# Attention values copied out unturned, scaled by their inverted sums on loading, and an SP list in a new order

## The chip, the core and the metric

One core of a Trainium2 chip runs the whole program. The metric is the device time of one execution in microseconds; the median of several runs is compared. A profile of one further execution gives the trace.

## What is computed

The input `x` has 8 batches of 1024 tokens with 256 features. `xn` is its layer norm. The result is `x + attention(xn) + linear(xn)`, where the linear part quantises each token of `xn` to 8 bits, multiplies by an int8 matrix and scales back, and the attention is:

```python
q = (x @ Wq.T).reshape(n, s, 16, 16)           # 16 heads of 16
k = (x @ Wk.T).reshape(n, s, 8, 16)            # 8 key heads, each shared by 2 heads
v = (x @ Wv.T).reshape(n, s, 8, 16)
energy = einsum('nqhd,nkhd->nhqk', q, k) + alibi(s, s)   # -|i - j| times a slope for each head
attn = softmax(energy / 4, axis=-1)
out = einsum('nhqk,nkhd->nqhd', attn, v).reshape(n, s, 256) @ Wo.T + bo
```

## The kernel before

**Units.** The work of attention is cut into 64 units: unit `u` is key head `u % 8` of batch `u // 8`, with the two query heads that share it (`e` = 0, 1) and all 1024 tokens. The 64 token tiles of 128 (layer norm, q, k, v, the linear part) are made ahead of the units that need them: eleven at the start, two in each odd unit up to unit 53. Odd units from 9 on also project two tiles of finished attention (`outputs`), whose operands `load_att_t` brings from DRAM. So the code alternates between short even units and longer odd ones; the last odd units make no tiles.

**A unit on TensorE.** A unit has eight steps `c`, one for each block of 128 keys. In a step PE computes four `col_half` results (keys by queries) into a ring of three PSUM banks; ScalarE takes the exp of each out of its bank into `probs`; GpSimd multiplies the diagonal block by ALiBi's share (`weigh_near`); and two steps later `pv_block` multiplies `probs` by the values into `ps_pv`, with a column of ones so that row 16 of each group holds the sum of the exps. Between these PE computes two blocks of row scores (queries by keys, `half_row_block`) into two banks `ps_row`, ahead of their use: in unit `u` the blocks 0 to 7 belong to head 1 of unit `u + 1`, the blocks 8 to 15 to head 0 of unit `u + 2`. VectorE reduces each to the rows' maxima (`reduce_block`), and PE may fill a bank again only when it has been reduced. The maxima go, through GpSimd and a turn on VectorE (`turn_max`), back into the query operand by small DMAs (`place_max`), which PE waits for at the start of the next unit.

**Operands.** q and k are split into three bf16 parts in DRAM (`store_parts`); `load_set` brings the rows of a unit into one of four slots with thirteen DMAs. `load_again` copies 64 of these rows to partitions 64 to 127 (`k_again`, `q_again`), so that `half_row_block` can use both halves of PE at once. The first set of each batch after the first is a *late set* (units 8, 16, ... 56): its last tile is made only three units before. Its loads stand at the end of SP's list of that unit (an odd one) and its `load_again` at the end of the next unit's list (an even one). Its head-0 blocks use `row_block`, which needs no copy.

**Values out.** When a unit's last `pv_block` is done, VectorE turns `ps_pv` into `pv_turned` (`turn_pv`), inverts the sums (`find_rsum`), multiplies (`norm`, on GpSimd in even units) and turns back (`turn_back`); `store_att` puts the result into `att_dram`. `ps_pv` is free for the next unit's first `pv_block` after `turn_pv`. The last batch's tiles are projected by `project_last` in the last two units and at the end, straight into the then unused `ps_row` banks.

**Order.** Nothing is scheduled automatically. Each engine runs its list in the order in which it is written, and waits at semaphores. All DMAs are issued by SP from one list; the order of the calls in its `unit` is the order of issue, and a DMA whose wait is not met holds up everything behind it.

Of the kernel before, what the change touches and what calls it, by code (L numbers as in the profile page):

```python
# [35 lines left out]
P = 128  # L36
# [27 lines left out]
V_COLS = 32  # L64
LN_EPS = 1e-5
# [6 lines left out]
PAIR = 2  # L72
# [20 lines left out]
FIRST_ROWS = K_LOADS + Q_LOADS + ALIBI_LOADS  # L93
# [45 lines left out]
def ring_places():  # L139
# [3 lines left out]
    for u in range(UNITS):  # L143
        f = flags_of(u)
        for c in range(BLOCKS):
            items = [(u, c, e, h) for e in range(GROUP) for h in range(2)]
            if c == 1:
                items += [(u, "outputs", t % PAIR) for t in f["proj"] or f["made"]]
                items += [(u, "qkv", t % PAIR) for t in f["made"]]
            for item in items:  # L150
                places[item] = len(places)
# [38 lines left out]
def build(nc, x, x_t, wqk_t, wv_t, wo_t, wo_last_t, w8_t, w_scale, bias_attn, bias_lin, q_alibi, k_alibi, diag,  # L190
          eye, parts_dram, token_dram, att_dram, out):
    ctx = ExitStack()
    with ctx:
# [58 lines left out]
        rsum = sb("rsum", [P, HALF // TURN])  # L252
        att_normed = sb("att_normed", [P, HALF // 2])
        att_unit = sb("att_unit", [P, HALF // 2])
        att_t = sb("att_t", [P, 2, EC, P])
        att_last = sb("att_last", [P, EC, SEQ])
# [12 lines left out]
        parts_more = parts_more.bitcast(BF16).rearrange("p (b m n) -> p b m n", b=2, m=PARTS)  # L269

# [92 lines left out]
        pv_read = sem("pv_read")  # L363
        rsum_ready = sem("rsum_ready")
        norm_done = sem("norm_done")
        att_unit_ready = sem("att_unit_ready")
        att_stored = sem("att_stored")
        att_t_loaded = [sem(f"att_t_loaded{i}") for i in range(2)]
# [62 lines left out]
        def _(sp):  # L431
# [20 lines left out]
            def load_set(u, slot):  # L452
# [3 lines left out]
                def rows(dst, chunk, row, pick, loaded=set_loaded[slot]):  # L456
                    for at, q_parts, k_parts in PAIRS:
# [16 lines left out]

                pairs = KV_HEADS // (QK_CHUNKS - 1)
                rows(k_set[:, slot, :], QK_CHUNKS - 1, g * HEAD_DIM, "k",
                     first_rows_loaded if u == 0 else set_loaded[slot])
                for e in range(GROUP):
                    rows(q_set[:, slot, e, :], g // pairs, (g % pairs * GROUP + e) * HEAD_DIM, "q",
                         first_rows_loaded if u == 0 and e == 0 else set_loaded[slot])  # L480
# [29 lines left out]
            def store_att(u):  # L510

                wait(sp, att_unit_ready, u + 1)
                for e in range(GROUP):
                    dst = att_dram[bass.ds((u % KV_HEADS * GROUP + e) * HEAD_DIM, HEAD_DIM),
                                   bass.ds(u // KV_HEADS * SEQ, SEQ)]
# [974 lines left out]
```

## Time and profile before

| | |
|---|---|
| median of 3 runs | 1607.19 us (1605.15 to 1607.93) |
| profiled execution | 1606.43 us, of which the span from first to last instruction is 1604.5 us |
| TensorE (PE) busy | 1507.3 us, 94% of the span |
| VectorE (DVE) busy | 1394.1 us, 87% |
| ScalarE (ACT) busy | 1183.8 us, 74% |
| GpSimd (POOL) busy | 1073.4 us, 67% |
| mean granted clock of TensorE | 0.978 of full speed |

Times in the rows are microseconds from the start of the span unless they are marked ns. A line such as L999 is a line of the kernel. Matmuls are pipelined and their ends are modelled, so a busy PE is not PE at its peak. SPq is the queue of SyncE, which issues the DMAs. What stands in brackets is the idle time of the engine before the instruction, and what ended it.

### The profile page before, as it was taken

The page shows a single profiled execution, that of the slowest core. Times are in us where ns is not written, and L with a number is a line of the kernel's source. Part 1 is how long each engine was busy: PE and PEld are TensorE (multiplying, and loading weights), DVE is VectorE, ACT ScalarE, POOL GpSimd, SP SyncE. Part 2 cuts the span into 40 slices and gives each one's busy share as a digit, 9 for nine tenths or more (in the row PEclk, how much of TensorE's full clock was granted, in tenths as well). Part 3 has the DMA queues.
Part 4 walks back from the last instruction along what each step waited for, and adds up shares of the span by engine and source line. Part 5 has one row for each costly group of instructions (what it writes and reads, how often), then busy time and mean ns, then how long its engine had stood idle before and what let it go on. Part 6 is the DMA issues. An engine that isn't in the chain of part 4 may idle for free.

```text
span 1604.5 us, 42517 instructions
## 1 busy us (share of the span) xinstructions
PE 1507.3 (94%) x16284; PEld 584.2 (36%) x16284; DVE 1394.1 (87%) x1698; ACT 1183.8 (74%) x2331; POOL 1073.4 (67%) x1627
## 2 busy tenths in 40 slices
PE   5789989999899998999989999899998999899999
PEld 5323323333333333333333334333333333233333
DVE  6889989999799997999979999799987988899991
ACT  3467777777687775887757887677776777688885
POOL 6457877777688875787757787577785776433332
PEclk9899999999999999999999999999999999999999
DMA  6423233343324333333333333333333332212211
GB/s 169 130 62 84 71 99 79 89 98 84 105 72 106 96 79 98 93 93 101 84 84 95 103 90 90 89 94 97 94 86 85 95 85 69 80 44 70 70 42 61
DMA packets 197291, 140.98 MB, mean 88 GB/s; under 512 B 107040, under 2 KB 165728, under 8 KB 197088
## 3 DMA queue, kind: packets, MB, share of 16 engines
q1 hardware_dynamic: 197088, 138.27, 33.0%
q8 instruction: 129, 2.11, 0.6%
q14 instruction: 74, 0.61, 0.1%
HBM read 81.40 MB, written 35.63 MB: 73 GB/s over the span
## 4 chain that ended last, share of the span: by engine, by line
PE 53%; DVE 31%; issue 8%; SPq 4%; DMA 3%; POOL 0%; ACT 0%; POOLq 0%; ACTq 0%
DVE row_max L999 29%; PE ps_ring L1279 17%; PE ps_pv L1355 15%; PE ps_row L1296 11%; PE ps_ring L1395 4%; PE ps_ring L1415 3%; DMA q_again<-q 2%; PE ps_ring L1398 1%; DVE pv_turned L1039 1%; PE ps_row L1279 1%; PE ps_ring L1409 1%; SPq L497 1%; PE ps_row L1387 1%; SPq L464 0%; DMA base<-x 0%
## 5 line engine op out<-in xcount | busy, mean ns | idle before, releaser
L999 DVE TENSOR_REDUCE row_max<-ps_row 128x1 f32<-128x1024 f32 x1024 | 1199.2, 1213 | 153.8 <-PE ps_row L1298 138.5
L1171 ACT ACTIVATE probs<-ps_ring 128x512 f32<-128x512 f32 x2048 | 1083.7, 601 | 284.8 <-PE ps_ring L1279 282.3
L1279 PE MATMUL ps_ring<-q,k 122*32 122x512 bf16 x8192 | 639.2, 385 | 5.6 <-DMA q<-neg_max_t 4.7
L762 POOL TENSOR_TENSOR probs<-probs,near 128x256 f32<-128x256 f32 x512 | 374.2, 731 | 368.5 <-ACT probs L1171 362.8
L1355 PE MATMUL ps_pv<-probs,v_unit 128*32 128x512 f32 x4096 | 537.9, 601 | 0.0
L1279 PEld LDWEIGHTS ps_ring<-q,k 122*32 122x32 bf16 x8192 | 216.5, 95 | 511.7 <-ACT probs L1171 324.6
L1296 PE MATMUL ps_row<-k,q 64*128 64x512 bf16 x944 | 329.7, 390 | 68.1 <-DMA q_again<-q 43.2
L1298 PE MATMUL ps_row<-k_again,q_again 64*128 64x512 bf16 x944 | 329.6, 390 | 0.0
L1296 PEld LDWEIGHTS ps_row<-k,q 64*128 64x128 bf16 x944 | 83.9, 93 | 362.9 <-issue 197.8
L1355 PEld LDWEIGHTS ps_pv<-probs,v_unit 128*32 128x32 f32 x4096 | 125.2, 110 | 55.1 <-issue 9.1
L1298 PEld LDWEIGHTS ps_row<-k_again,q_again 64*128 64x128 bf16 x944 | 83.8, 93 | 0.0
L817 POOL CAST parts<-qk 128x384 bf16<-128x384 f32 x53 | 26.6, 502 | 83.4 <-ACT qk L1180 83.4
L1395 PE MATMUL ps_ring<-xn_t,wqk 128*128 128x128 f32 x636 | 79.9, 275 | 0.5 <-ACT probs L1171 0.5
L1395 PEld LDWEIGHTS ps_ring<-xn_t,wqk 128*128 128x128 f32 x636 | 77.0, 192 | 2.5 <-ACT probs L1171 1.3
L1039 DVE STREAM_TRANSPOSE pv_turned<-ps_pv 128x512 f32<-128x512 f32 x64 | 45.2, 706 | 28.4 <-PE ps_pv L1355 28.4
L809 POOL TENSOR_SCALAR xq_t<-xround 128x256 bf16<-128x256 f32 x53 | 57.3, 1081 | 4.5
L801 POOL TENSOR_SCALAR xround<-xt_step 128x256 f32<-128x256 f32 x53 | 57.0, 1075 | 4.5
L689 POOL TENSOR_TENSOR parts<-rest,parts 128x384 bf16<-128x384 f32 x59 | 54.1, 917 | 7.2 <-ACT parts L1127 3.0
L1177 ACT ACTIVATE v_all<-ps_ring 128x128 f32<-128x128 f32 x53 | 14.7, 277 | 58.5 <-PE ps_ring L1398 58.5
L1415 PE MATMUL ps_ring<-wo,att_t 128*128 128x256 f32 x224 | 57.4, 382 | 0.0
L1279 PE MATMUL ps_row<-k,q 120*32 120x512 bf16 x640 | 45.3, 390 | 11.7 <-issue 8.9
L819 POOL TENSOR_TENSOR rest<-qk,parts 128x384 f32<-128x384 f32 x53 | 48.5, 916 | 4.3
(84 smaller groups left out, 1009.1 us busy)
## 6 DMA issues: line engine op xcount, KB each, us to landing
parts_dram<-parts SPq DMA_DIRECT2D x59, 288.0 KB, 3.3
q_again<-q SPq DMA_DIRECT2D x63, 256.0 KB, 3.4
token_b<-token_dram SPq DMA_DIRECT2D x53, 256.0 KB, 4.0
q<-parts_dram SPq DMA_DIRECT2D x128, 96.0 KB
k<-parts_dram SPq DMA_DIRECT2D x256, 32.0 KB
q<-parts_dram SPq DMA_DIRECT2D x128, 64.0 KB
att_dram<-att_unit SPq DMA_DIRECT2D x126, 64.0 KB
att_t<-att_dram SPq DMA_DIRECT2D x56, 128.0 KB, 2.9
```

Of the source, the lines that this page charges most:

```text
L762: pool.tensor_tensor(here, here, near[:, u % KV_HEADS, :].rearrange("p (e n) -> p e n", e=GROUP), ALU.mult).then_inc(weighted, 1)
L801: pool.tensor_scalar(xround[:, :], xt_step[:, 1, :, :].rearrange("p c n -> p (c n)"), Q_MAX, ROUND, ALU.min, ALU.add).then_inc(xt_rounded, 1)
L809: pool.tensor_scalar(xq_t[:, t % TURNED, :, :].rearrange("p c n -> p (c n)"), xround[:, :], -ROUND, -Q_MAX - 1, ALU.add, ALU.max).then_inc ...
L999: dve.tensor_reduce(row_max[:, par, e, qb:qb + 1], ps_row[qb % 2][:, :], AX_X, ALU.max, negate=True).then_inc(row_max_found, 1)
L1039: dve.transpose(pv_turned[:, :], ps_pv[:, :]).then_inc(pv_read, 1)
L1171: act.activation(probs[:, c % PBUFS, e, h * HALF:(h + 1) * HALF], ring_bank(u, c, e, h), ACT.Exp, scale=SCALE).then_inc(ring_freed, 1)
L1279: mm = pe.matmul(to[at, :], weights[:, at], moving, start=start, stop=stop)
L1296: pe.matmul(ps_row[qb % 2][:, 0:HALF], q_set[0:ROW_K, slot, e, at], k_set[0:ROW_K, slot, 0:HALF], start=True, stop=True)
L1298: pe.matmul(ps_row[qb % 2][:, HALF:SEQ], q_again[ROW_K:2 * ROW_K, u % AGAIN, e, at], k_again[ROW_K:2 * ROW_K, u % AGAIN, :], start=True, s ...
L1355: mm = pe.matmul(ps_pv[32 * j:32 * j + 32, :], v_unit[:, par, c, :], probs[:, c % PBUFS, j // 2, (j % 2) * HALF:(j % 2 + 1) * HALF], start ...
L1395: pe.matmul(bank[:, m * P:(m + 1) * P], wqk[:, c, m * P:(m + 1) * P], xn_t[:, t % TURNED, c, :], start=(c == 0), stop=(c == EC - 1))
L1415: mm = pe.matmul(bank[:, EMBED:2 * EMBED], att_t[:, t % 2, c, :], wo[:, c, :], start=(c == 0), stop=(c == EC - 1))
```

## The change

- ScalarE copies `ps_pv` to `att_raw` as it is (`keep_pv`); `store_att` stores that with its row of sums. `load_sums` brings the sums back spread over 128 partitions, VectorE inverts them (`find_rsum`, before block 13 of the next unit), `store_rsum` stores them. The two tiles to be projected are loaded together (`load_att_t`), with the inverted sums broadcast (`load_att_r`), and GpSimd multiplies (`share`) in step 0 of the projecting unit. The turns and `norm` are left only for the last unit; the last batch's values are multiplied on VectorE (`share_last`).
- On SP, `load_again` of a late set moves near the top of the next unit's list, and late sets use `half_row_block` like the others. `row_block`, now for the first units alone, uses 64 rows in place of 120, and the rows that it needs of set 0 are loaded first. `place_max(0, 0)` and `load_again(1, 1)` move up in the list at the start.
- In step 1 of odd units `qkv_whole` stands before `outputs`, on PE and ScalarE.

```diff
@@ SP: functions
-                wait(sp, att_unit_ready, u + 1)
-                for e in range(GROUP):
...
+                sp.wait_ge(pv_read, u + 1)
+                sp.dma_start(att_dram[u // KV_HEADS, u % KV_HEADS].rearrange("e h r n -> (e h r) n"),
+                             att_raw[:, u % 2, :]).then_inc(att_stored[u % 2], 16)
+            def load_sums(u):
+                sp.wait_ge(att_stored[u % 2], 16 * (u // 2 + 1))
+                wait(sp, rsum_ready, u - 1)
+                sp.dma_start(sums[:, u % 2, :],
+                             att_dram[u // KV_HEADS, u % KV_HEADS, :, :, HEAD_DIM, :].rearrange(
+                                 "e h (k n) -> (e h) k n", n=SUMS)).then_inc(sums_loaded[u % 2], 16)
+            def store_rsum(u):
+                sp.wait_ge(rsum_ready, u + 1)
+                sp.dma_start(rsum_dram[u // KV_HEADS, u % KV_HEADS].rearrange(
+                    "e (k n) -> (e k) n", n=SUMS), rsum[:, u % 2, :]).then_inc(rsum_stored[u % 2], 16)
+            def load_att_r(t):
+                b, at = t // BLOCKS, t % BLOCKS * P
+                wait_units(rsum_stored, (b + 1) * KV_HEADS)
+                for c in range(EC):
+                    sp.dma_start(att_r[:, c, :],
...
@@ SP: at the start
             load_set(2, 2)
+            load_again(1, 1)
             sp.dma_start(wo[:, :, :], wo_t.rearrange("(c p) n -> p c n", p=P)).then_inc(
...
             load_token(PREP_AHEAD)
-            load_again(1, 1)
+            place_max(0, 0)
             load_again(2, 2)
-            place_max(0, 0)
@@ SP: unit
                     load_xt(u + 2 + PREP_AHEAD)
+                if u + 2 < UNITS and late_set(u + 2):
+                    load_again(u + 2, (u + 2) % SETS)
+                if f["prev"]:
+                    store_att(u - 1)
                 if f["row_set"] and not late_set(u + 3):
                     next_set(u + 3)
-                if u % PAIR == 1:
-                    store_att(u - 1)
                 for t in f["normed"]:
                     store_token(t)
...
+                if f["prev"]:
+                    load_sums(u - 1)
...
                 if not f["last"]:
                     place_max(u + 1, (u + 1) % SETS)
-                if f["prev"] and u % PAIR == 0:
-                    store_att(u - 1)
-                for t in f["next_att"]:
-                    load_att_t(t, t % 2)
+                for t in f["next_att"][:1]:
+                    load_att_t(t)
+                if f["prev"] and not f["last"]:
+                    store_rsum(u - 1)
                 if f["row_set"]:
                     if late_set(u + 3):
                         next_set(u + 3)
                     else:
                         load_again(u + 3, (u + 3) % SETS)
-                if u + 2 < UNITS and late_set(u + 2):
-                    load_again(u + 2, (u + 2) % SETS)
+                for t in f["next_att"][:1]:
+                    load_att_r(t)
@@ GpSimd
+            def share(t):
+                pool.wait_ge(att_t_loaded, 16 * 2 * EC * (t // PAIR + 1))
+                pool.tensor_tensor(att_t[:, :, :], att_t[:, :, :], att_r[:, :, :],
+                                   ALU.mult).then_inc(att_t_ready, 1)
...
-                    if c == 3 and f["prev"] and u % PAIR == 0:
-                        norm(u - 1)
+                    if c == 0:
+                        for t in f["proj"][:1]:
+                            share(t)
@@ VectorE
+                dve.wait_ge(sums_loaded[u % 2], 16 * (u // 2 + 1))
+                wait(dve, rsum_stored[u % 2], 16 * (u // 2))
+                dve.reciprocal(rsum[:, u % 2, :], sums[:, u % 2, :]).then_inc(rsum_ready, 1)
...
                     for i in (2 * c, 2 * c + 1):
+                        if i == 13 and f["prev"]:
+                            find_rsum(u - 1)
                         if i < BLOCKS and f["row_heads"] >= 1:
                             reduce_block(u + 1, (u + 1) % 2, 1, i)
                         if i >= BLOCKS and f["row_heads"] >= 2:
                             reduce_block(u + 2, u % 2, 0, i - BLOCKS)
-                        if i == 3 and f["prev"]:
-                            turn_pv(u - 1)
...
+                    if c == 3 and u == UNITS - 2:
+                        share_last(0, P)
@@ ScalarE
+            def keep_pv(u):
+                act.wait_ge(pv_done, BLOCKS * (u + 1))
+                wait(act, att_stored[u % 2], 16 * (u // 2))
+                act.activation(att_raw[:, u % 2, :], ps_pv[:, :], ACT.Copy).then_inc(pv_read, 1)
...
+                    if c == 1 and f["prev"]:
+                        keep_pv(u - 1)
@@ TensorE
-                        if not late_set(u + 2):
-                            wait_again(u + 2)
-                    if late_set(u + 2):
-                        row_block(u + 2, (u + 2) % SETS, 0, i - BLOCKS)
-                    else:
-                        half_row_block(u + 2, (u + 2) % SETS, 0, i - BLOCKS)
+                        wait_again(u + 2)
+                    half_row_block(u + 2, (u + 2) % SETS, 0, i - BLOCKS)
...
-            project_last(1, P - GROUP * HEAD_DIM, 2)
             pv_block(UNITS - 1, (UNITS - 1) % 2, BLOCKS - 1)
-            for i in range(3, BLOCKS):
+            for i in range(BLOCKS):
                 project_last(1, P - GROUP * HEAD_DIM, i)
```

## Rows read from the trace of the kernel before

**Rows 1.** The chain of work that ended last, shares by engine.
```profile
PE 53%; DVE 31%; issue 8%; SPq 4%; DMA 3%; POOL 0%; ACT 0%; POOLq 0%; ACTq 0%
```
**Rows 2.** Timeline of VectorE in an even unit: start, duration, instruction.
```profile
552.32 4.73 DVE L999 TENSOR_REDUCE row_max<-ps_row 128x1 f32<-128x1024 f32 x4 [0.28 <-PE ps_row L1298]
...
559.83 0.23 DVE L1046 RECIPROCAL rsum<-pv_turned 128x16 f32<-128x16 f32 x1
...
562.56 2.36 DVE L999 TENSOR_REDUCE row_max<-ps_row 128x1 f32<-128x1024 f32 x2 [0.29 <-PE ps_row L1298]
...
567.57 2.35 DVE L999 TENSOR_REDUCE row_max<-ps_row 128x1 f32<-128x1024 f32 x2 [0.28 <-PE ps_row L1298]
569.84 0.43 DVE L1065 STREAM_TRANSPOSE att_unit<-att_normed 128x256 f32<-128x256 f32 x1
```
**Rows 3.** List of waits: total, times, longest.
```profile
PE ps_row L1296 <- DMA q_again<-q: 43.2, 7, 7.2
```
**Rows 4.** Windows: length, busy engines, clock, DMA; sum of the seven late pairs.
```profile
537.29:583.54 46.25, 45.58 (x494) 17.70 (x492) 43.27 (x53) 36.52 (x73) 35.41 (x54) 1.00 0.34 91
1452.45:1494.77 42.32, 41.66 (x458) 13.70 (x456) 40.23 (x41) 34.60 (x67) 14.82 (x25) 1.00 0.25 69
...
sum 377.79, PE 330.84 PEld 126.25 DVE 300.44 ACT 254.79 POOL 238.30; mean PE 47.26 PEld 18.04 DVE 42.92 ACT 36.40 POOL 34.04
```
**Rows 5.** Timeline of SP's queue around a late set.
```profile
595.50 0.62 SPq L468 DMA_DIRECT2D k<-parts_dram  x1
...
601.74 0.83 SPq L488 DMA_DIRECT2D k<-k_alibi  x2
...
603.50 0.45 SPq L555 DMA_DIRECT2D xt<-x_t  x1
...
622.09 0.59 SPq L499 DMA_DIRECT2D q_again<-q  x1
```
**Rows 6.** Timeline of TensorE in the same stretch.
```profile
608.27 1.04 PE L1279 MATMUL ps_row<-k,q 120*32 120x512 bf16 x16
...
625.91 0.60 PE L1296 MATMUL ps_row<-k,q 64*128 64x512 bf16 x1 [6.99 <-DMA q_again<-q]
```
**Rows 7.** Timeline of SP's queue: a set's first DMA in a quiet stretch.
```profile
1469.48 0.69 SPq L468 DMA_DIRECT2D k<-parts_dram  x1
```
**Rows 8.** Windows at the end of that set; DMA share is the last but one.
```profile
1478.50:1479.50 1.00, 1.00 (x20) 0.29 (x12) 1.00 (x2) 0.69 (x3) 0.81 (x3) 1.00 0.15 57
1479.50:1480.00 0.50, 0.50 (x9) 0.10 (x2) 0.50 (x2) 0.50 (x2) 0.00 (x0) 1.00 0.05 16
```
**Rows 9.** DMA issues: count, size, median us from issue to landing.
```profile
q_again<-q SPq DMA_DIRECT2D x63, 256.0 KB, 3.4
...
token_dram<-token SPq DMA_DIRECT2D x53, 2.0 KB, 3.9
```
**Rows 10.** Timelines of ScalarE and SP in the even unit of rows 2.
```profile
556.57 2.06 ACT L1171 ACTIVATE probs<-ps_ring 128x512 f32<-128x512 f32 x4 [0.48 <-PE ps_ring L1279]
...
556.90 0.69 SPq L468 DMA_DIRECT2D k<-parts_dram  x1
...
564.95 0.35 SPq L568 DMA_DIRECT2D token_b<-token_dram  x1
```
**Rows 11.** Timeline of GpSimd and TensorE in an odd unit that makes no tiles.
```profile
1490.25 0.73 POOL L762 TENSOR_TENSOR probs<-probs,near 128x256 f32<-128x256 f32 x1 [1.17 <-ACT probs L1171]
...
1491.87 1.99 PE L1415 MATMUL ps_ring<-wo,att_t 128*128 128x256 f32 x8
```
**Rows 12.** Timelines of SP and TensorE at the start of unit 0.
```profile
64.70 0.34 SPq L568 DMA_DIRECT2D token_b<-token_dram  x1
...
67.72 3.17 SPq L506 DMA_DIRECT2D q<-neg_max_t  x4
...
72.12 1.04 PE L1279 MATMUL ps_ring<-q,k 122*32 122x512 bf16 x8 [4.74 <-DMA q<-neg_max_t]
```
**Rows 13.** Timeline of TensorE at the end.
```profile
1595.14 2.43 PE L1387 MATMUL ps_row<-wo,att_last 96*128 96x256 f32 x10
```

More of the change, by code:

```diff
@@ L92 @@
 ALIBI_LOADS = 2
-FIRST_ROWS = K_LOADS + Q_LOADS + ALIBI_LOADS
+NEAR_PAIRS = tuple(pair for pair in PAIRS if pair[0] < ROW_K)
+FAR_PAIRS = tuple(pair for pair in PAIRS if pair[0] >= ROW_K)
+FIRST_ROWS = 2 * len(NEAR_PAIRS) + ALIBI_LOADS
 def made_unit(t):
@@ L454, in load_set, with rows @@
                 g, tok = u % KV_HEADS, (u // KV_HEADS) * SEQ
-                def rows(dst, chunk, row, pick, loaded=set_loaded[slot]):
-                    for at, q_parts, k_parts in PAIRS:
+                def rows(dst, chunk, row, pick, pairs=PAIRS, loaded=set_loaded[slot]):
+                    for at, q_parts, k_parts in pairs:
                         use = q_parts if pick == "q" else k_parts
@@ new lines, in wait_units, with heads_of, load_att_t @@
+            def wait_units(stored, units):
+                for i in range(2):
+                    sp.wait_ge(stored[i], 16 * len(range(i, units, 2)))
+            def heads_of(c):
+                return slice(c * (KV_HEADS // EC), (c + 1) * (KV_HEADS // EC))
+            def load_att_t(t):
+                b, half, at = t // BLOCKS, t % BLOCKS // (BLOCKS // 2), t % (BLOCKS // 2) * P
+                wait_units(att_stored, (b + 1) * KV_HEADS)
+                if t >= PAIR:
+                    wait_filled(sp, projected_unit(t - PAIR), "outputs", 1)
+                for c in range(EC):
+                    sp.dma_start(att_t[:, c, :],
+                                 att_dram[b, heads_of(c), :, half, 0:HEAD_DIM, at:at + PAIR * P].rearrange(
+                                     "g e d n -> (g e) d n")).then_inc(att_t_loaded, 16)
@@ L850, in unit @@
             def unit(u, f):
-                t = u + PREP_AHEAD
+                turned = u + PREP_AHEAD
                 for c in range(BLOCKS):
@@ L1077, in unit @@
                             reduce_block(u + 2, u % 2, 0, i - BLOCKS)
-                        if i == 3 and f["prev"]:
-                            turn_pv(u - 1)
-                        if i == at_sums and f["prev"]:
-                            find_rsum(u - 1)
-                        if i == at_norm and f["prev"] and not apart:
-                            norm(u - 1)
-                        if i == SLOTS - 3 and apart:
-                            turn_back(u - 1)
                     if c == 1:
```

182 lines of the change are left out of this document (90 added, 92 removed).

## The prediction

> **What bounds the kernel now.** I read the chain of work that ended last first: 53% of it is TensorE, 31% VectorE [rows 1]. In steady work TensorE and VectorE alternate: PE fills two `ps_row` banks, VectorE reduces them, and a bank must be read before it is filled again. Eight blocks undisturbed would take 10.02 us, twice the 5.01 us for four between 562.56 and 567.57 [rows 2]; with `turn_pv` and `find_rsum` among them, from 552.32 to 562.56, they take 10.24. So VectorE's extra work costs only 0.22 us there, since part of it falls into idle time that the handshake leaves anyway.
>
> Then the list of waits: PE waited 43.2 us for `q_again`, seven times, up to 7.2 [rows 3]. Windows of two units say where: an ordinary pair takes 46.25 us, a pair late in the kernel that makes no tile 42.32, and the seven pairs in which a batch's first set arrives late 377.79 together [rows 4]. Six ordinary pairs and one short one are 319.82, so the seven lose 58.0 us, 8.3 each. SP's list and PE's tell how [rows 5, 6]: the late set's loads are issued from 595.50 to 602.6, but its second copy follows only at 622.09, behind another set, `place_max`, `store_att`, `load_att_t` and the next set's copy; PE, which reached the blocks at about 618.9, starts them at 625.91, and its matmuls then run 0.60 us instead of 0.39 for a while.
>
> Last, the landing of a set. Its thirteen DMAs begin at 1469.48 and traffic ends at about 1479.7 [rows 7, 8]; in the tail only 0.15 of 16 engines are busy, 2.4 engines. So a set lands 10.2 us after its first issue, and a few engines set that.
>
> **The change, part by part.** *Late copies.* `load_again` of the late set now stands near the top of SP's list of the even unit, but it waits for the set. The set's loads come behind `store_rsum` in the unit before, which adds one small issue of 0.45 us: first issue 595.95 [rows 5], landed 10.2 later, 606.15. SP is there by 604.4 and waits, as everything behind it does. The k copy's issue takes 0.59 like the q copy's, so the q copy starts at 606.8 and lands 3.4 later (median, [rows 9]): 610.2. Now the even unit's head-0 blocks need that copy too, at about 608.1 (the old block, which read the set directly, ran at 608.27 [rows 6], less 0.2 for VectorE's relief). PE waits 2.1 us; bounds 0.7 (set landed when SP gets there) and 3.1 (the copy takes 3.8, as at 622.09 to 625.9, and its set 0.6 more). I add 0.6 for slow matmuls after the stall (0 to 1.7).
>
> *Values out.* `turn_pv`, `norm` and `turn_back` leave VectorE. In an odd unit they hide behind the tile work of PE, so they give nothing. In an even one they give 0.22 [rows 2] and about 0.2 for `turn_back`, whose 0.43 us at 569.84 stands ahead of a reduction that PE waits for: together -0.42 a pair. ScalarE gets a copy of 128x512; like an exp of that size it takes 0.6, placed after the exps of c = 1, where ScalarE has idle time: four exps take 2.06 us [rows 10] of the 2.5 that a step of c lasts. A ring bank comes free up to 0.25 late: 0.1 taken (0 to 0.25). GpSimd loses a product in even units and gains, in odd ones, `share` on 128x512; it waits for others in most steps, so only PE's wait for `share` counts (below).
>
> *Sums back.* This is the new wait. `find_rsum` moves to just before block 13 and waits for `load_sums`. Everything queued behind it on VectorE waits too, first the reduction of block 13, and PE's block 15 waits for that; so what it lasts is PE's. The reciprocal itself (0.23) costs about 0.2 in each unit, 0.4 a pair. Now its data. In an even unit the copy of the values starts when the exp begun at 556.57 is done, 557.1, ends at 557.7; `store_att` takes 0.4 of SP's time, so `next_set` starts at 558.3, 1.4 later than before [rows 10]. `load_sums` comes behind its thirteen DMAs, 8.05 later, 566.35 (as the token load at 564.95 stood to 556.90). If it goes through the engines of the tail, it lands with the set, 558.3 + 10.2, plus 0.4 for its own small packets: 568.9. VectorE arrives at 567.57 + 1.18 - 0.2 = 568.55 [rows 2]. Stall 0.4. Bounds: 0, if it does not queue behind the tail; 1.7, if it takes 3.9 us from its issue as the token store does, the row nearest to it in packet size [rows 9]. I take 0.4, nearest to the set's own landing, which rows show most directly. An ordinary pair so costs -0.42 + 0.4 + 0.1 + 0.4 = +0.5 (-0.1 to +2.0); 24 of them, +12.
>
> The Trainium skill (DMA: Bandwidth & Descriptors, "Why a DMA increments its semaphore by 16 and not by 1") says that an SP transfer is split over as many engines, up to 16, as divide the outermost dimensions of both sides, and takes the lowest-numbered. Loads with two or three parts outermost would then sit on engines 0 to 2, which the 0.15 share bears out, and the sums, four rows outermost, on 0 to 3, behind them. By that rule the stall is the 0.4 taken; without it the sums could land at once, and the sum would be 10 us lower.
>
> In a late pair the set behind the copies starts at about 608.0 and its sums land at 608.0 + 10.2 + 0.4, and 0.6 for the copies' data ahead of it: 619.2. VectorE arrives a pair later than above, 568.55 + 46.25, plus the stalls of 2.1 and 0.6: 617.5. It waits 1.7. New loss of a late pair: 2.1 + 0.6 + 1.7 and the common +0.1 = 4.5 for 8.3 before; seven give -26.6.
>
> `place_max` of an even unit now comes behind `store_att` and `load_sums` too, at about 567.1. From its first issue to PE's start it took 4.4 us where PE stood waiting, 67.72 to 72.12 [rows 12], so 571.5. PE's next unit starts two steps of c after that of block 12, about 571.5 and the stall of 0.4. I take 0 (0 to 0.5). `store_rsum` and `load_att_r` stand at the list's end; once a batch `load_att_r` must see the last sums stored (about 3.9 [rows 9]), and behind it wait `store_out` and the next unit's x loads. SP then stood before `store_att`, which waits for the copy 6.4 us into the unit anyhow: 0.
>
> *Projection.* PE makes qkv first, so `share` is covered by it in units that make tiles. Five odd units at the end make none: GpSimd's product of c = 0 ends at 1490.98 there, `share` takes twice its 0.73, to 1492.4, and PE wanted the operands at 1491.87 [rows 11]. 0.6 each, and about 1 more where the batch's last sums are only just stored: +4.
>
> *Start.* Fewer first rows let PE begin 2 to 3 us earlier, but SP's list governs unit 0. `place_max` (67.72) came 3.0 after the token load (64.70), behind two pairs of copies [rows 12]. The first blocks' 64 rows instead of 120 change nothing by themselves: the columns are the same. One pair moves ahead of the token's store and delays it by 1.2, the other behind: -1.5 (-3 to 0).
>
> *End.* Eight of the last products instead of five stand behind the last values, at 0.24 an instruction with two each [rows 13], less what no longer stands between earlier matmuls; and `share_last(0)`, 128x1024 on VectorE, delays the first projection by about its 1.2 us (a reduction of that size takes 1.18). Together +2 (0 to 4).
>
> **Sum.** -26.6 + 12 - 1.5 + 4 + 2 = -10.1. The profiled execution took 1606.43 us (span 1604.5); its sum is 1596.3. The median of the runs is 0.8 above it, so I forecast 1597 for a median.
>
> **Rivals.** *The sums come late (slower).* At 3.9 us from issue the even units' stall is 1.7, 1.3 more than taken; over 31 pairs that is +40, 1637. It decides from a stall of 0.7 on, where the ten microseconds are spent. For it: the small packets, and a load of values stored in the same unit. Against it: the set in front lands at 568.5, and nothing else is queued there.
>
> *The rows' cover holds (much faster).* Copies land when PE needs them and sums pass the tail: late pairs keep 0.5, 7 x 7.8 = 55 gained, ordinary ones cost +0.1, +2; with start, projection and end 1607.2 - 55 + 2 + 4.5 = 1559. For it: the copies leave some 15 us earlier than the 622.09 of before [rows 5]. Against it: they cannot leave before 606.15.
>
> *It cancels (no change).* One late wait becomes three smaller ones, stalls of 2.7 and 2.6 in the late unit leave 5.9 of 8.3: -17 + 12 + 4.5, 1607. For it: VectorE and PE stand in lockstep, so neither stall hides the other.
>
> **Chances.** Forecast 0.38 (1588 to 1603), sums late 0.34, cover 0.15, cancels 0.13. What a measurement can tell from no change is about 0.2%, 3.2 us: faster 0.38 + 0.15 = 0.53, same 0.13, slower 0.34. The range reaches to 1565, which leaves out half of the third case, and to 1630, leaving out about a third of the second.
>
> **What the profile after would show.** PE's waits for `q_again`: seven of about 2 us, where 43.2 stood. VectorE waiting for `sums` before `find_rsum`: 0.4 in even units, nothing in odd ones. Pairs of 46.7 in place of 46.25. ScalarE about 38 us busier, VectorE less busy by what it turned (0.43 a unit for `turn_back` alone [rows 2]), with hardly any gain from that. Were VectorE's wait over 0.7, or PE's for the copies over 4, I would be wrong by sign; were PE to wait for `set_loaded` at the start of odd units, I would have placed `place_max` wrongly.

## The result, and the profile of the changed kernel

The changed kernel takes 1646.3 us (median of four runs, 1638.6 to 1653.0) where the kernel before took 1607.6 in the same comparison: a ratio of 1.024, 95% interval 1.019 to 1.029. It is 2.4% slower; the forecast was 1597, range 1565 to 1630. The profiled execution of the changed kernel took 1638.56 us, with a span of 1636.8 where that of before was 1604.5. It was the quickest of the four: the two traces differ by 32.3 us, the medians by 38.7.

The page of the changed kernel, busy time by engine and the chain that ended last, stands against [rows 1]:

```profile
PE 1512.9 (92%) x15948; PEld 578.4 (35%) x15948; DVE 1328.3 (81%) x1542; ACT 1214.6 (74%) x2394; POOL 1095.7 (67%) x1624
...
PE 31%; DVE 17%; SPq 17%; POOL 13%; issue 11%; DMA 9%; ACT 2%; POOLq 0%; ACTq 0%; DVEq 0%
```

VectorE is 65.8 us less busy, as the change says, and the kernel is slower all the same. SP's queue, 4% of the chain before, is now 17%, and DMA went from 3% to 9%: the chain runs through transfers. The list of waits (total, times, longest) says which; the last line is from the kernel before:

```profile
DVE rsum L1099 <- DMA sums<-att_dram: 66.8, 31, 18.4
PE ps_row L1348 <- DVE row_max L1060: 59.4, 65, 3.7
...
PE ps_row L1348 <- issue: 21.3, 7, 3.5
...
PE ps_ring L1461 <- POOL att_t L815: 5.1, 5, 2.5
```
```profile
PE ps_row L1296 <- DVE row_max L999: 11.0, 39, 1.9
```

VectorE waited 31 times for the sums: in thirty even units 48.4 us together, from 0.71 to 3.40, and 18.4 in the last unit, where nobody waits for it. The second line is what PE paid for it: 59.4 us of waits for a reduction, of which the kernel before had 11.0 as well, and the other 48.4 are what VectorE waited in the even units. The third, named "issue" here, stands where late sets are first used: seven waits for late copies, 3.0 each where [rows 3] had 6.2. The fourth is PE's wait for `share`. One even unit in detail, on SP, VectorE and PE:

```profile
714.95 0.69 SPq L481 DMA_DIRECT2D k<-parts_dram  x1
...
722.23 0.59 SPq L539 DMA_DIRECT2D sums<-att_dram  x1
```
```profile
721.64 3.61 DVE L1060 TENSOR_REDUCE row_max<-ps_row 128x1 f32<-128x1024 f32 x3
726.38 0.25 DVE L1099 RECIPROCAL rsum<-sums 128x16 f32<-128x16 f32 x1 [1.13 <-DMA sums<-att_dram]
```
```profile
727.76 0.39 PE L1348 MATMUL ps_row<-k,q 64*128 64x512 bf16 x1 [1.16 <-DVE row_max L1060]
```

The set's first load goes out at 714.95, the sums at 722.23, VectorE asks for them at 725.25 (726.38 less 1.13), 10.30 us after the set's first issue, and gets them 11.43 after it. The 1.13 us are PE's as well, 1.16, behind the reduction that VectorE could not start. In most other even units VectorE came at the same 10.30, and in all thirty the sums landed 11.0 to 12.8 us after the first issue. At the end of the kernel, with no set ahead, the same load took no more than 2.05 us from issue to use (SP and VectorE):

```profile
1610.76 0.55 SPq L539 DMA_DIRECT2D sums<-att_dram  x1
```
```profile
1612.81 0.25 DVE L1099 RECIPROCAL rsum<-sums 128x16 f32<-128x16 f32 x1 [18.37 <-DMA sums<-att_dram]
```

By pairs (windows; as in [rows 4], an odd unit and the even one behind it, here cut where `ps_pv` is read): an ordinary one, a late one and one without tiles:

```profile
735.11:782.40 47.29, 45.73 (x494) 17.57 (x494) 41.30 (x49) 37.50 (x76) 36.23 (x54) 1.00 0.39 104
782.40:836.68 54.28, 47.16 (x494) 17.64 (x494) 41.33 (x48) 37.60 (x76) 35.92 (x54) 0.97 0.36 95
...
1519.43:1562.90 43.47, 41.43 (x456) 13.33 (x454) 37.96 (x36) 35.60 (x69) 14.62 (x25) 1.00 0.27 78
```

Cut where a unit's `ps_pv` is read (the same place in both traces), the two traces part as follows. Twenty pairs that make tiles and are not late: +31.6 us, 1.6 each. Seven late pairs: -9.4. The last four pairs: +9.9. Start -0.2, end +0.4. Sum +32.3, the difference of the spans. The same kernel profiled once more, in a run of 1644.3 us (e17), parts in +33.4, -11.3, +12.2, +3.4 and +0.4: of the 5.7 us that its span is longer, 3.6 are the start. Late pairs still lose 7.0 us each against ordinary pairs of before (46.25, the first of the seven 45.26), where they lost 8.4. In the pair of the second row, on SP, PE and in two windows,

```profile
801.14 0.62 SPq L481 DMA_DIRECT2D k<-parts_dram  x1
...
812.89 0.59 SPq L518 DMA_DIRECT2D q_again<-q  x1
```
```profile
816.43 0.37 PE L1348 MATMUL ps_row<-k,q 64*128 64x512 bf16 x1 [2.96 <-issue]
...
827.88 0.39 PE L1348 MATMUL ps_row<-k,q 64*128 64x512 bf16 x1 [3.67 <-DVE row_max L1060]
```
```profile
826.00:829.00 3.00, 1.12 (x14) 0.38 (x17) 2.51 (x4) 0.35 (x1) 1.00 (x1) 0.95 0.37 99
829.00:832.00 3.00, 3.00 (x24) 0.63 (x16) 1.15 (x2) 1.72 (x4) 0.80 (x2) 0.50 0.68 188
```

PE waits 2.96 us for the copy, then 3.67 behind VectorE's wait for the sums (the copies had pushed back the next set, and the sums with it), and after that wait the granted clock is 0.50 of full speed (1.2 GHz) for some 3 us.

### The profile page after: what moved, and what is told of

Its sections match the earlier page's. It is cut to its first block, busy times and chain, and to the rows that moved or that the text cites. A ratio compares the mean times of both kernels' runs of the same rounds, so it can differ in the third digit from the quotient of the medians.

```text
span 1636.8 us, 41809 instructions
## 1 busy us (share of the span) xinstructions
PE 1512.9 (92%) x15948; PEld 578.4 (35%) x15948; DVE 1328.3 (81%) x1542; ACT 1214.6 (74%) x2394; POOL 1095.7 (67%) x1624
## 4 chain that ended last, share of the span: by engine, by line
PE 31%; DVE 17%; SPq 17%; POOL 13%; issue 11%; DMA 9%; ACT 2%; POOLq 0%; ACTq 0%; DVEq 0%
DVE row_max L1060 15%; PE ps_ring L1331 9%; PE ps_pv L1407 8%; DMA sums<-att_dram 6%; PE ps_row L1348 5%; SPq L477 5%; SPq L481 4%; POOL probs L822 4%; PE ps_ring L1441 3%; SPq L485 3%; PE ps_ring L1461 2%; DMA k<-k_alibi 2%; SPq L507 1%; SPq L525 1%; POOL parts L754 1%
## 5 line engine op out<-in xcount | busy, mean ns | idle before, releaser
L1348 PE MATMUL ps_row<-k,q 64*128 64x512 bf16 x1000 | 346.4, 389 | 94.2 <-DVE row_max L1060 59.4
L1350 PE MATMUL ps_row<-k_again,q_again 64*128 64x512 bf16 x1000 | 346.6, 389 | 0.0
L1348 PEld LDWEIGHTS ps_row<-k,q 64*128 64x128 bf16 x1000 | 88.9, 93 | 391.4 <-issue 226.8
L1350 PEld LDWEIGHTS ps_row<-k_again,q_again 64*128 64x128 bf16 x1000 | 89.1, 93 | 0.0
L1099 DVE RECIPROCAL rsum<-sums 128x16 f32<-128x16 f32 x63 | 15.6, 247 | 66.8 <-DMA sums<-att_dram 66.8
L849 POOL TENSOR_TENSOR xn_t<-xt_step,token_b 128x256 f32<-128x256 f32 x53 | 45.7, 863 | 4.2
L844 POOL TENSOR_TENSOR xt_step<-xt,token_b 128x256 f32<-128x256 f32 x53 | 47.3, 893 | 0.0
```

What stands on the lines that cost most here:

```text
L1348: pe.matmul(ps_row[qb % 2][:, 0:HALF], q_set[0:ROW_K, slot, e, at], k_set[0:ROW_K, slot, 0:HALF], start=True, stop=True)
L1350: pe.matmul(ps_row[qb % 2][:, HALF:SEQ], q_again[ROW_K:2 * ROW_K, u % AGAIN, e, at], k_again[ROW_K:2 * ROW_K, u % AGAIN, :], start=True, s ...
```

## Experiments

Medians are of the runs of each kernel; the ratio is to the kernel before on the same chip, with its 95% interval.

| run | median us | ratio |
|---|---|---|
| e1 sums inverted before block 15 | 1610.9 | 1.002 (1.001 to 1.003) |
| e2 sums loaded inside the set | 1600.4 | 0.996 (0.994 to 0.998) |
| e3 sums left out | 1596.4 | 0.993 (0.991 to 0.996) |
| e4 before, late copies alone | 1568.9 | 0.976 (0.973 to 0.978) |
| e5 before, copies up, old block | 1573.2 | 0.980 (0.977 to 0.982) |
| e7 e2 with the old block | 1613.9 | 1.003 (1.002 to 1.005) |
| e8 e2 with the maxima inside too | 1595.5 | 0.992 (0.991 to 0.994) |
| e9 e2, inverted before block 9 | 1608.1 | 1.000 (0.998 to 1.001) |
| e10 before, copies behind the maxima | 1549.8 | 0.964 (0.962 to 0.966) |
| e11 before, copies ahead of the maxima | 1557.8 | 0.969 (0.967 to 0.971) |
| e12 e8 with the copies as in e10 | 1593.0 | 0.990 (0.987 to 0.994) |
| e13 before, start alone | 1613.8 | 1.003 (1.002 to 1.004) |
| e14 before, blocks of 64 rows alone | 1612.3 | 1.004 (1.002 to 1.005) |
| e15 e10 with the start's moves | 1551.7 | 0.965 (0.964 to 0.967) |
| e16, e18 changed, blocks of 120 rows | 1639.7, 1641.6 | 1.020 (1.019 to 1.022), 1.022 (1.020 to 1.024) |
| e17 changed, again | 1645.4 | 1.023 (1.021 to 1.026) |

**The stall on the sums.** My theory: it is the loss. Rival: it hides another. Three edits of the changed kernel take it away in different ways.

```diff
@@ e1, VectorE
-                        if i == 13 and f["prev"]:
+                        if i == 15 and f["prev"]:
@@ e2, SP: load_set, called by next_set with the unit whose sums it is to load
                     rows(k_set[:, slot, :], QK_CHUNKS - 1, g * HEAD_DIM, "k")
+                    if between is not None:
+                        load_sums(between)
                     for e in range(GROUP):
@@ e3, SP: unit
-                if f["prev"]:
+                if u in (1, 2):
                     load_sums(u - 1)
@@ e3, VectorE: find_rsum
-                dve.wait_ge(sums_loaded[u % 2], 16 * (u // 2 + 1))
+                dve.wait_ge(sums_loaded[u % 2], 16)
```

e3 scales by old sums; it is there for its time alone.

> Changed kernel, but VectorE inverts the sums before block 15 instead of before block 13. Theory (the sums are late for VectorE): it arrives two reductions, about 2.45 us, later, that is 12.75 us after the set's first issue where it came at 10.30; the sums were there after 11.0 to 12.8. So of the 48.4 us that VectorE waited in thirty even units about 4 stay, and the slow matmuls behind the longer stalls go too: 1590 to 1597 us. Rival (the stall only hides another loss: place_max, the copy on ScalarE or the longer list on SP would be late next): the time stays above 1625 and another wait of about 1 us in each even unit takes the place of this one.

> Changed kernel, but load_sums is issued inside the set, behind its five k loads and ahead of its eight other DMAs, some 5 us earlier than before. Theory: the sums then land well before VectorE comes at 10.30 us after the set's first issue, its wait of 48.4 us falls to under 3 except where no set is issued ahead of them, and the time is 1588 to 1597. Rival (what is late is the round trip through DRAM itself, or the added transfers slow the set): the waits shrink by less than half, or PE waits longer for the sets, and the time stays above 1615.

> Changed kernel with the sums loaded only in units 1 and 2; every later unit inverts what lies there, so the shares are those of old sums. It prices the loads and VectorE's wait for them together. Theory: 48.4 us of waits go, and with them the slow matmuls behind the longer ones, some 8 pairs at 1.5 to 2 us: 1575 to 1590. Rival (the loss lies in ScalarE's copy, in share or in the list): above 1625.

All three kernels lose the stall wholly (in e1 and e2 VectorE waits for the sums only in the last unit, in e3 once, 2.3 us in unit 2, where it still loads them), and are 35 to 50 us faster than the changed one. In e3, without the load and its wait, ordinary pairs take 46.3: what is left of the values' way costs a pair 0.1 us. VectorE's relief does show in even units: from a unit's first column matmul to the next unit's they take 20.13 us for 20.26 before. Odd units, where the turns had been hidden behind tile work and the inversion now stands among the reductions, take 26.18 for 25.98. But each run stays above its theory's range, because something else is late next. In e3 that is the late pairs, which still lose 5.4 us (waits for copies of 3.1 and slow matmuls behind them), and the start (below). In e1 the stores of the inverted sums come some 2 us later, and with them the late set, whose loads stand behind `store_rsum`: PE waits for late copies 38.0 us instead of 21.3, and for `share` 11.3 instead of 5.1. Waits of e1:

```profile
PE ps_row L1348 <- issue: 38.0, 7, 6.8
...
PE ps_ring L1461 <- POOL att_t L815: 11.3, 5, 3.2
```

Waits of e2:

```profile
PEld ps_ring L1334 <- DMA q<-neg_max_t: 23.6, 26, 2.1
...
DVE rsum L1102 <- DMA sums<-att_dram: 18.3, 1, 18.3
...
PE ps_ring L1334 <- DMA q<-neg_max_t: 7.9, 12, 1.4
```

In e2 it is the maxima: PE waits for `place_max` at the start of odd units. In the changed kernel the stall covered that (0.3 us in all). e8 tests it, e9 where the sums' delay comes from.

```diff
@@ e8, on top of e2, SP: load_set, in even units
+                if ahead is not None:
+                    place_max(ahead, ahead % SETS)
                 if u >= SETS - 1:
                     load_alibi(u, slot)
@@ e9, on top of e2, VectorE
-                        if i == 13 and f["prev"]:
+                        if i == 9 and f["prev"]:
```

> Changed kernel with load_sums inside the set, and in even units place_max also inside it, ahead of the two ALiBi loads and the token load. In the run with the sums inside the set VectorE no longer waited for them, but PE's engine and its weight loads waited 7.9 and 23.6 us for the maxima at the start of odd units, and ordinary pairs still varied from 46.3 to 47.5. Theory (the maxima are what is late next): those waits fall under 5 us together, ordinary pairs take 46.3 and the time is 8 to 12 us lower than with the sums alone inside, 1588 to 1593. Rival (the variation is that of the clock or of the transfers themselves): within 3 us of 1600.

> Changed kernel with load_sums inside the set, but VectorE asks for the sums before block 9, some 5.0 us sooner, so that it shows when they land: it comes about 5.2 us after the set's first issue, 2.6 after the issue of the sums. Theory (the sums were late because they lay behind the rest of the set; nearly alone they took 2.05 us at the end of the kernel): they land 2.0 to 2.8 us after their issue, VectorE waits less than 0.3 in most even units, and the time is within 6 us of the run before block 13, 1595 to 1606. Rival (4 us from issue to landing is what such a small load takes anywhere): VectorE waits 1.4 us in each even unit, and the time is 1625 to 1645.

e8: the weight loads' waits for maxima fall from 23.6 us to 7.7, PE's from 7.9 to 2.7, even units in ordinary pairs all take 20.1, and 4.9 us are gained, half of what I expected: twenty ordinary pairs gained 6.4 in the profiled runs, but PE's waits for `share` grew from 5.8 to 8.1 and the last four pairs took 2.5 more. e9: in 18 of the thirty even units the sums were there when VectorE asked, 2.6 us or less after their issue; in 12 it waited, 15.7 us together, and got them 2.05 to 3.07 us after their issue. Behind the whole set it was 2.8 to 4.9, 4.2 in the mean. The theory holds for the landing, though the waits were more than expected and the time lies above its range. The wait of e9, in which 18.5 is the last unit's:

```profile
DVE rsum L1102 <- DMA sums<-att_dram: 34.8, 14, 18.5
```

**The late copies.** In the changed kernel they gave 9.4 us instead of 26.6. Theory: the sums behind them took the rest. So that part alone, in the kernel before:

```diff
@@ e4, SP: unit, near its top; e5 has this edit alone
+                if u + 2 < UNITS and late_set(u + 2):
+                    load_again(u + 2, (u + 2) % SETS)
                 if f["row_set"] and not late_set(u + 3):
                     next_set(u + 3)
...
-                if u + 2 < UNITS and late_set(u + 2):
-                    load_again(u + 2, (u + 2) % SETS)
@@ e4, PE: late sets on half_row_block, as in the change
```

> Kernel before with one part of the change alone: load_again of a late set near the top of the next unit's list, and late sets on half_row_block. Nothing of the sums. Theory (of a late pair's loss in the changed kernel only the 3.0 us wait for the copies belongs to the copies, the rest to the sums behind the next set): late pairs lose 3 to 4 us in place of 8.3, the time is 1570 to 1581. Rival (the copies ahead of the next set cost a late pair some 7 us by themselves, through that set and the unit that waits for it): 1593 to 1603.

> Kernel before with load_again of a late set near the top of the next unit's list and nothing else: its head-0 blocks keep row_block, which reads the set itself. With half_row_block added (the run with the late copies alone) late pairs still lost 3.7 us, of which 2.1 are PE's wait for the copies. Theory (the change of block made that wait; without it the copies are needed only a unit later): late pairs lose about 0.5 us, what four steps of row_block took more (2.61 against 2.50 us each), so some 22 us less than that run: 1544 to 1552. Rival (SP, standing at the top of its list for the set, makes what is behind it late, the maxima above all): 1558 to 1569.

> Changed kernel with load_sums inside the set (as in the run of that name) and row_block kept for the head-0 blocks of late sets. Theory: the late pairs lose PE's wait of 3.1 us for the copies and the slow matmuls behind it, 31 us in all: 1567 to 1574. Rival (in a late unit the set behind the copies, and the maxima behind that set, are late next, and take half of it back): 1580 to 1592.

e4 is 2.4% faster than before, 1 us under its theory's range: late pairs lose 3.0 us, of which 2.1 are the wait for the copies:

```profile
PE ps_row L1296 <- issue: 14.6, 7, 3.0
```

So a part of the change gains 39 us alone, and is buried in a whole that loses 39. But my theory that the copies only had to be taken off PE's path fell in e5 and e7: both lie above even their rivals' ranges, e7 14 us above its partner e2, e5 4 us above e4 (their intervals just overlap). Waits of e5:

```profile
PE ps_ring L1279 <- DMA q<-neg_max_t: 20.9, 8, 5.3
```

One of the eight is the first unit's; the others, 15.6 us together, are new. SP, at the top of its list, stands for the late set, and everything behind comes late, the maxima above all. With `half_row_block` PE waited for the copies meanwhile and saw little of it (2.1 us in e4). In e7 the waits for the maxima are 32.0 us in all.

So the copies belong neither at the top (SP stands) nor at the end (they leave at 622.09, [rows 5]), but in between. The next three move them there:

```diff
@@ e10, kernel before, SP: unit (removed at the list's end)
                 if not f["last"]:
                     place_max(u + 1, (u + 1) % SETS)
+                if u + 2 < UNITS and late_set(u + 2):
+                    load_again(u + 2, (u + 2) % SETS)
@@ e11: the same two lines ahead of place_max
@@ e12: e8, with late sets as in e10 and load_again where place_max stood
```

> Kernel before with one call moved: load_again of a late set stands directly behind place_max of the next unit, ahead of store_att, load_att_t and the other set's copy; its head-0 blocks keep row_block. Theory (at the list's top the copies make SP stand for the set and the maxima come late; at its end they come 7 us late themselves; in between neither does): the copies are issued about 6 us sooner than in the kernel before, 614.9 and 615.5 where they were 621.5 and 622.1, and land at 619 to 619.6, PE comes at 618.9 and waits up to 0.7 us; no wait for the maxima. Late pairs lose 0.5 to 1.5 us instead of 8.3: 1554 to 1563. Rival (wherever they stand, copies and maxima of that unit share a transfer time that comes to some 3 us): 1567 to 1575, like the two runs with the copies at the top.

> As the run with the copies behind the maxima, but directly ahead of place_max. Theory: the copies then land at about 617, before PE wants them at 618.9; the maxima go out 1.2 us later, from 613.4, and are there at about 617.8, when PE wants them at 618.1; late pairs lose about 0.5 us: 1551 to 1560, not over 3 us from the run with the copies behind. Rival (the copies' 384 KB delay the maxima behind them by 2 us or more): PE waits 1 to 3 us for the maxima in late units, 1562 to 1575.

> Changed kernel with the sums inside the set, the maxima inside it in even units, and late sets as in the run of the kernel before with the copies behind the maxima (row_block for head 0, load_again where place_max stood). Theory (with its three waits taken away the values' new way costs almost nothing and gives nothing): ordinary pairs 46.3, late pairs 46.9 to 48, about 5 us for share at the end; 1562 to 1572, some 8 us above the kernel before with the copies so placed. Rival (the values' way has a cost of its own that the waits hid): over 1580.

e10 is 3.6% faster than before, by one call moved, and beats both kernels. A window of a late pair, and what is left of its waits:

```profile
745.78:792.37 46.59, 46.13 (x541) 18.61 (x540) 43.37 (x55) 36.50 (x72) 35.51 (x54) 1.00 0.37 93
```
```profile
PE ps_ring L1279 <- DMA q<-neg_max_t: 5.4, 1, 5.4
...
PEld ps_row L1296 <- DMA q_again<-q: 2.7, 3, 1.2
...
PE ps_row L1296 <- DMA q_again<-q: 1.3, 2, 0.7
```

The wait of 5.4 is the first unit's. Late pairs lose 0.5 us, PE waits for the copies only twice, 1.3 us together, and the granted clock stays at full speed (2.4 GHz) from 76 us to the end of the span. The median lies 4 us below the theory's range. In e11 the maxima wait behind the copies (PE 11.6 us, 4.5 of it in the first unit): its expected time came, but 8 us from e10 where I said at most 3, so the rival's mechanism is there too, at about 1 us a pair. e12 misses: 1593 for 1562 to 1572. The sums and their store stand ahead of the copies, they leave later, and PE waits for them again:

```profile
PE ps_row L1353 <- DMA q_again<-q: 15.8, 6, 3.1
```

Counted from where `ps_pv` is read at the start of the odd unit, its copies leave 1.6 to 3.3 us later than those of e10, and its late pairs lose 4.4 us. So the values' new way has a cost besides the stall after all: what it adds to SP's list delays what is behind. That is the rival's answer, at least in late units. Of the 47.5 us between the profiled runs of e12 and e10 the late pairs are 27.2, the last four pairs, with their waits for `share`, 10.8, the start 5.5 and ordinary pairs 3.6. The new way is not all of the 27.2: late sets use `row_block` with 64 rows here, as in e7, and e14 below prices that at 0.7 a pair.

**The start.** It was forecast at -1.5 and is -0.2 in the profiled run, but 3 to 4 us in most other profiled runs with the same start.

```diff
@@ e14, kernel before, PE: row_block, and k_set alike (e13 has this, the first rows first, and SP's moves)
-                q = q_set[0:SET_K, slot, e, qb * P:(qb + 1) * P]
+                q = q_set[0:ROW_K, slot, e, qb * P:(qb + 1) * P]
...
@@ e15: e10, with load_again(1, 1) and place_max(0, 0) moved up
@@ e16, e18: changed kernel, with SET_K here again and the first loads in the old order
```

> Kernel before with the start of the change alone: near rows of the first set ahead of its far rows, row_block on 64 rows, load_again(1, 1) and place_max(0, 0) further up. The forecast took -1.5 us (-3 to 0). Theory (the first unit waits for its maxima, which go out sooner): PE's wait of 4.7 us for the first maxima falls under 2 and the time is 1604 to 1606.5. Rival (the time until the first set's rows decide, and that differs more from run to run than by this): no difference that three rounds can tell, within 2 us of 1607.4.

> Kernel before with row_block on 64 rows instead of 120 and nothing else (it serves the three first blocks of eight at the start and the head-0 blocks of late sets). In the run with the start alone TensorE's granted clock stayed at 0.50 from 35 to 80 us, and 42.0 us lay between its first row block and its first column block, where the kernel before rose to 1.00 at 43 us and took 34.9, a wait of 4.7 for the maxima among them; and a step of c with row_block in late units took 2.81 us instead of 2.61. Theory (the 64 rows do both): the clock stays low here too, the start takes 39 to 43 us between the same two blocks, late pairs 0.5 to 1 us more, and the time is 1612 to 1619. Rival (the clock hangs on the order of the loads and the earlier start): clock and late steps as in the kernel before, 1605 to 1609.

> The run of the kernel before with the copies behind the maxima (1549.8), and of the start only the two moves in SP's list: load_again(1, 1) and place_max(0, 0) further up, with blocks of 120 rows. Theory: PE's wait of 5.4 us for the first maxima shrinks by what the moves bring place_max forward, 1 to 3 us, and nothing else changes: 1546.5 to 1549. Rival (the copy that now stands ahead of the token's store delays the token load, and with it the maxima behind): 1549.5 to 1552.

Both e13 and e14 are 5 to 6 us slower than before, so the 64 rows alone do it; of e13's two expectations neither came. In the profiled run of e14, the quickest of its six, the start takes 1.2 us more and the late pairs 4.7; in that of e13 3.3 and 5.2. Two ways show. First the clock, in windows of the start of the kernel before and of e14 (the third number from the right):

```profile
50.00:55.00 5.00, 4.67 (x55) 2.32 (x52) 5.00 (x6) 2.15 (x8) 3.49 (x5) 1.00 0.44 133
```
```profile
50.00:55.00 5.00, 5.00 (x38) 2.31 (x31) 3.51 (x4) 1.07 (x3) 2.03 (x4) 0.50 0.43 131
```

It is at 1.2 GHz when the first row block starts, in all traces. With 120 rows it is at full speed by 42 to 45 us in all eight, 4 to 7 us after that start; with 64 by 61 or 62 us in three (the changed kernel, e1, e14) and by 80 or 81 in the other eight. In e14 it takes 37.2 us from the first row block to the first column block, not the 39 to 43 expected, for 34.9 before. Second, in late units, weight loads and matmuls of one step, before and in e14:

```profile
608.06 0.32 PEld L1279 LDWEIGHTS ps_row<-k,q 120*32 120x32 bf16 x8
```
```profile
609.50 0.55 PEld L1279 LDWEIGHTS ps_row<-k,q 64*32 64x32 bf16 x16 [0.42 <-issue]
...
612.31 0.12 PEld L1279 LDWEIGHTS ps_row<-k,q 64*32 64x32 bf16 x8 [0.42 <-issue]
```

The 120-row weights are loaded from 608.06, 0.21 ahead of their matmuls at 608.27 [rows 6]; those of 64 rows begin only with their matmuls, 609.50. A step takes 2.81 us where it took 2.61, and late pairs lose 0.7 more. e15 gives the rival's answer: the moved copy goes out ahead of the token's store, and the first maxima come no earlier (PE waits 6.1 us for them, 5.4 in e10); nothing is gained.

> Changed kernel with row_block on 120 rows and the first set loaded in the old order; all else as changed. Theory (64 rows at the start keep the clock low, for 25 to 45 us, and differently from run to run): from the first row block to the first column block it takes 30 to 33 us instead of 37.5 in the profiled run and 42 in six others, the time is 1636 to 1642. Rival (what the low clock costs is what PE would have waited for maxima anyway): 1644 to 1649, as changed.

> The changed kernel itself, once more, beside the run with blocks of 120 rows. Its four times lay between 1638.6 and 1653.0, those of the kernel with 120 rows between 1637.2 and 1642.0. Theory (64 rows keep the clock low at the start, for 25 us in the profiled run, for 42 in six other kernels with the same start): the median lies 4 to 8 us above that with 120 rows on the same chip, and from first row block to first column block it takes 37 or 42 us. Rival (the spread comes from the stalls on the sums, in both alike): within 3 us of each other.

> The changed kernel with blocks of 120 rows and the old order of the first loads, once more, beside the changed kernel on the same chip. Theory: 4 to 8 us under the changed kernel, its times within 6 us of each other. Rival: within 3 us of it, and as widely spread.

First row block and first column block of e17 and of e18, on PE:

```profile
35.07 1.90 PE L1331 MATMUL ps_row<-k,q 64*32 64x512 bf16 x16 [6.50 <-issue]
...
77.06 1.04 PE L1331 MATMUL ps_ring<-q,k 122*32 122x512 bf16 x8
```
```profile
38.39 1.90 PE L1323 MATMUL ps_row<-k,q 120*32 120x512 bf16 x16 [10.44 <-issue]
...
72.18 1.04 PE L1323 MATMUL ps_ring<-q,k 122*32 122x512 bf16 x8 [3.23 <-DMA q<-neg_max_t]
```

That is 42.0 us against 33.8, less the 3.3 by which the 64 rows let PE begin sooner. In e16 it is 35.3, not the 30 to 33 expected, with 5.7 of it a wait for the maxima, against 37.5 and 0.3 in the first trace of the changed kernel: part of what the slow clock costs is time in which PE would have waited, as e16's rival says. In time it should be some 5 us between e17 and e18; measured are 4, and 7 between the changed kernel and e16, with intervals that overlap. So its size in the changed kernel stays open, and so does the cause of the spread of the changed kernel's runs, which is there with 120 rows too in e18 (1637.7 to 1648.0).

## Why the prediction was wrong, step by step

- **What bounds the kernel**: right. PE and VectorE alternate; the seven late waits were worth 8.4 us each, and e10 gets nearly all of it back.
- **Values out**: right in size. Without the stall the forecast's terms for an ordinary pair make +0.1; e3 measured 46.3 for 46.25, and in its parts too (even units 0.13 shorter, odd ones 0.20 longer) it came as the terms have it.
- **Sums**: the step that failed, by its size. "Stall 0.4" was 1.6 in the mean of thirty units, the smallest 0.71. VectorE's arrival was right: 10.25 us after the set's first issue forecast, 10.30 measured. Wrong was the landing, 10.2 for the set, taken from one late in the kernel with little other traffic [rows 7, 8], and 0.4 for the sums' own packets, 10.6 together; they were there after 11.0 to 12.8, 11.7 in the mean. The 0.4 stands in no row. Even in the last units, which make no tiles, the sums took 11.0 to 11.2, and 11.2 to 12.8 in units with more traffic; that the traffic is the reason is likely, but no run tests it. The order behind it was right: e2 and e9 show that what stands ahead of the sums in the list delays them. The Trainium skill's rule (DMA: Bandwidth & Descriptors, "Why a DMA increments its semaphore by 16 and not by 1"), by which the sums lie behind the set's tail, agrees with that; on which engines they lay no run here shows. The upper bound from the token store, 1.7, was nearer: it goes by 3.9 us from issue to landing, and the mean measured from issue to use is 4.2. The rival that named it, *the sums come late*, had this stall and gave 1637. That the profiled run took 1638.6 is partly luck: the rival has ordinary pairs at +1.8 each, which took 1.6, and the late ones at -17.5 together, which gave 9.4. The median is 1646.3.
- **Late copies**: mechanism right, size wrong for the same reason. 2.1 forecast, 3.0 measured; SP waits for the set before it issues the copies, and the k copy left 10.9 to 11.7 us after the set's first issue in the seven units, not 10.2. With the sums (1.7 forecast, 2.3 measured) and slow matmuls, more than the 0.6 taken, a late pair loses 7.0 instead of 4.5.
- **`place_max`**, taken as 0: 0.3 us in this kernel, because the stall hid it; with the stall gone some 5 us (e8). What would be late next was not asked there, nor for the top of SP's list (e5).
- **Projection**: +4 forecast; PE waited 5.1 us for `share`, in five units. Right.
- **Start**: that the first blocks' 64 rows change nothing by themselves was wrong (e14). **End**: +2 forecast, +0.4.

Sum of the forecast -10.1, of the trace +32.3: 17 us more from the late pairs, 22 from the twenty ordinary ones (0.5 each was forecast), 4 from the last four; start and end cancel.

## What to carry to other kernels

When an in-order engine is to wait for a small load, price its landing from a stretch as loaded as the one where it will run, behind everything that its list puts ahead; if the margin is as thin as it was here, issue it ahead of the large group instead, as e2 does. In a list that is issued in order, a call whose wait is not met delays all behind it: look for the latest place at which it is still in time, not the earliest. And time each part of a change alone: here a part that gains 2.4% by itself was buried in a package that lost 2.4%, and with its one call better placed it gains 3.6%.

## What the hardware showed unexpectedly

- With row blocks of 64 rows instead of 120 and the same columns, begun at 35 to 37 us, the granted clock was at 1.2 GHz until 61 or 62 us in three traces and until 80 or 81 in eight; with 120 rows, begun at 37 to 40, it was at 2.4 GHz from 42 to 45 in all eight.
- Weights of 120 rows were loaded while matmuls of 122 rows ran; weights of 64 rows only from the start of their own matmuls, 0.2 us a step. The Trainium skill (TensorE: Matmul & The Clock Gate, "The mechanism") says that weight loads overlap running matmuls only when their row groups differ; the 120-row loads, whose rows the running matmuls use too, don't agree with that. They would agree with the background weight buffer that the same section names, but then the 64-row loads stay unexplained.
- An 8 KB load took 2.05 us from issue to use with nothing ahead of it (last unit), up to 3.07 behind five loads of a set (e9) and up to 4.9 behind thirteen (changed kernel).
